# Identity transposes on TensorE in three idle stretches of a graph-attention kernel

## The chip, the cores and the metric

The kernel runs on 1 core of one Trainium2 chip. The metric is the device time of one execution in microseconds (us). A core has the matrix engine TensorE (PE), the vector engine VectorE (DVE), the activation engine ScalarE (ACT), GpSimd (POOL) and SyncE (SP), which here only issues transfers. Each engine works through its own instructions in order and waits on semaphores for the others.

## The reference

The input is x of 2048 x 512 and a sparse normalised adjacency matrix of 2048 x 2048. Cut to what matters:

```
h = relu(layernorm(x))
# layer 0: A = (adj + adj.T) / 2 + I, scaled on both sides by deg ** -0.5
y = (Coefficient2 @ A_norm) @ h      # here Coefficient2 is adj itself
x = x + y
h = relu(layernorm(x))
# layer 1: attention with 8 heads of width 64
Wh = einsum('nf,hfd->hnd', h, W)
e  = leaky_relu(e_src[:, :, None] + e_dst[:, None, :], 0.2), -9e15 where adj is 0
att = softmax(e); out = elu(att @ Wh), then four dense layers 512-256-128-256-512
x = x + out
```

The kernel computes adj @ (A_norm @ h) in two products of 2048 x 2048 by 2048 x 512, instead of making the 2048 x 2048 product first.

## The kernel before

There are three blocks, one after the other. Between two blocks all engines meet at a barrier, so nothing of a block starts before everything of the one ahead is done.

**The first product** (`smooth_features`) makes G = A_norm @ h. It runs over 32 steps: a step takes one tile of 128 rows of adj plus its transpose against half of the columns (1024 of them), and multiplies it with one tile of h. The numbers are 32-bit; to keep precision each operand is cut into a high and a low part, and `split_product` issues three matmuls for one product (L73, L74, L75), 128 x 128 against 128 x 512 each. A step has 8 column blocks, one for each bank of PSUM, so 24 matmuls. TensorE waits at the start of step s for `lo_ready` (DVE has cut the low part of the matrix tile) and for `x_ready` (DVE has cut the low part of the feature tile, L298, which needs the node degree and so both halves of the tile from memory). The first four steps (`EARLY`) use rows while they are still being loaded and summed. VectorE's and ScalarE's order in this stretch is written out by hand. `deg_ready` is counted by DVE: its first count is the degree of tile 0 (L322), three counts a tile. `ident` is the 128 x 128 identity matrix, which POOL makes in the first two microseconds.

**The second product and the projection** (`spread_and_project`) make adj @ G in two halves of 16 steps with the same 24 matmuls a step, then the layer norm, the product with W (L73 to L75 again, now with `w_hi` and `w_lo`), with transposes of the features by TensorE (L1016) ahead of it, and the attention terms e (L1040, L1050, L1055 are small TensorE operations at the end of this block).

**The attention and the dense layers** (`attend_and_finish`) handle 16 rounds (4 pairs of heads by 4 groups of 512 rows). A round r on TensorE (`sum_up`) is three phases of 64 matmuls of 260 columns each:

- `q_phase` for the first head: matmuls L1593 into four banks. It reads q, a 0/1 tile that DVE makes (L1278, one for each of 16 column tiles), and `parts`, the features times the attention factors, cut in high and low by ACT and POOL (L1410, L1512). It waits for `first_lo` (POOL) and `q_ready` (DVE).
- `m_phase`: matmuls L1617 with the mask that ACT converts (`take_mask`, L1391). In round 0 it waits first for `second_lo` (DVE, L1287). Its four output banks are 4, 5, 0 and 1, and banks 0 and 1 are those of the q phase just ended, so the third matmul waits until ACT has copied the q sums out (`take_q_sums`, L1397). ACT issues in order: in round 0 the sums stand behind eight masks (L1391).
- `q_phase` for the second head.

The change adds TensorE instructions at the head of each block: ahead of `products(0, ...)` in the first and in the second, and ahead of everything else in the attention block. The sequence on all other engines stays, except for one semaphore count that POOL adds behind making `ident`.

Of the kernel before, what the change touches and what calls it, by code (L numbers as in the profile page):

```python
# [37 lines left out]
P = 128  # L38
# [32 lines left out]
def split_product(pe, acc, hi, lo, rhs_hi, rhs_lo, first):  # L71

    pe.matmul(acc, hi, rhs_hi, start=first, stop=False, skip_group_check=True)  # L73
    pe.matmul(acc, hi, rhs_lo, start=False, stop=False, skip_group_check=True)  # L74
    return pe.matmul(acc, lo, rhs_hi, start=False, stop=True, skip_group_check=True)  # L75


def if_set(eng, flag):
# [23 lines left out]
def smooth_features(nc, bank, ident, G, rows, rows_loaded, x, adj, adj_t):  # L102
# [5 lines left out]
    with ExitStack() as ctx:  # L108
# [3 lines left out]
        def sem(name):  # L112
            return ctx.enter_context(nc.semaphore(name))
# [39 lines left out]
        ident_zeroed = sem("ident_zeroed")  # L153
# [10 lines left out]
        deg_ready = sem("l0_deg_ready")  # L164
# [40 lines left out]
        with nc.Block() as block:  # L205
# [406 lines left out]
            @block.gpsimd  # L612
            def _(p):
                p.memset(ident[:], 0.0).then_inc(ident_zeroed, 1)
                p.wait_ge(ident_zeroed, 1)
                p.affine_select(out=ident[:], in_=ident[:], compare_op=ALU.not_equal, fill=1.0, base=0,
                                pattern=[[-1, P]], channel_multiplier=1)

            @block.tensor
            def _(pe):  # L620
                pe.sem_inc(slot_free, 2)

                def products(s, b, early=None, first=False, last=False, bank_free=None):
                    pe.wait_ge(lo_ready, s + 1)
                    if early is None:
                        pe.wait_ge(x_ready, s - EARLY + 1)
                    else:
                        pe.wait_ge(x_ready, early + 1)
                    right = ((x_hi[:, b, :], x_lo[:, b, :]) if early is None
                             else (early_hi[:, early, :], early_lo[:, early, :]))  # L630
                    for k in range(G8):
                        if bank_free is not None:
                            pe.wait_ge(bank_free, k + 1)
                        cols = slice(k * P, (k + 1) * P)
                        mm = split_product(pe, bank[k][:], s_hi[:, b, cols], s_lo[:, b, cols], *right, first)
                        if last and k < G8 - 1:
                            mm.then_inc(acc_done, 1)
                    mm.then_inc(slot_free, 1)

                for s in range(EARLY):  # L640
                    products(s, s % 2, s, s == 0, s == EARLY - 1)
                for s in range(EARLY, FIRST_NOW):
                    products(s, s % 2, s - EARLY, s == EARLY, False, part_kept if s == EARLY else None)
                products(FIRST_NOW, 0)
                with pe.Fori(0, (FIRST_LATE - FIRST_NOW) // 2 - 1) as j:
                    products(FIRST_NOW + 1 + 2 * j, 1)
                    products(FIRST_NOW + 2 + 2 * j, 0)
                products(FIRST_LATE - 1, 1, last=True)
                products(FIRST_LATE, 0, first=True, bank_free=g_done)
                with pe.Fori(0, (STEPS - FIRST_LATE) // 2 - 1) as j:  # L650
                    products(FIRST_LATE + 1 + 2 * j, 1)
                    products(FIRST_LATE + 2 + 2 * j, 0)
                products(STEPS - 1, 1, last=True)


def in_turns(count, *stages):

    for k in range(count + max(lag for _, lag in stages)):
        yield k
        for work, lag in stages:  # L660
            if 0 <= k - lag < count:
                work(k - lag, (k - lag) % 2)


def spread_and_project(nc, bank, G, rows, rows_loaded, x1, mask, wh, e, fac, neg_d, ident, x, adj_t, w, a1, a2,
# [3 lines left out]
    with ExitStack() as ctx:  # L669
# [78 lines left out]
        with nc.Block() as block:  # L748
# [235 lines left out]
            @block.tensor  # L984
            def _(pe):
                pe.sem_inc(slot_free, 2)

                def products(s, b, g, first, last):
                    pe.wait_ge(g_ready, s + 1)
                    pe.wait_ge(lo_ready, s + 1)  # L990
                    for k in range(G8):
                        if first and g == 1:
                            pe.wait_ge(x1_done, k + 1)
                        cols = slice(k * P, (k + 1) * P)
                        mm = split_product(pe, bank[k][:], a_hi[:, b, cols], a_lo[:, b, cols],
                                           g_hi[:, b, :], g_lo[:, b, :], first)
                        if last:
                            mm.then_inc(acc_done, 1)
                    if not last:
                        mm.then_inc(slot_free, 1)  # L1000

                for g in range(2):
                    products(T * g, 0, g, True, False)
                    with pe.Fori(0, T // 2 - 1) as j:
                        products(T * g + 2 * j + 1, 1, g, False, False)
                        products(T * g + 2 * j + 2, 0, g, False, False)
                    products(T * g + T - 1, 1, g, False, True)
                    if g == 0:
                        pe.wait_ge(acc_done, G8)
                        pe.sem_inc(slot_free, 1)  # L1010

                def turn(t, b):
                    pe.wait_ge(h_ready, t + 1)
                    for k in range(KC):
                        cols = slice(k * P, (k + 1) * P)
                        mm = pe.transpose(bank[b][:, cols], h2[:, b, cols], ident[:])  # L1016
                    mm.then_inc(turned, 1)

                def project(t, b):
                    pe.wait_ge(t_lo_ready, t + 1)  # L1020
                    pe.wait_ge(wh_ready, t + 1)
                    for k in range(KC):
                        cols = slice(k * P, (k + 1) * P)
                        mm = split_product(pe, bank[2 + b][:], g_hi[:, b, cols], g_lo[:, b, cols],
                                           w_hi[:, k, :], w_lo[:, k, :], k == 0)
                    mm.then_inc(wh_summed, 1)

                pe.wait_ge(x1_done, G8 + 4)
                pe.wait_ge(w_ready, 1)
                pe.sem_inc(turned, 2)  # L1030
                pe.sem_inc(wh_summed, 2)
                def turn_e(tiles):
                    for t in tiles:
                        q = t // 4
                        if t % 4 == 0 and q >= 2:
                            pe.wait_ge(e_copied, q - 1)
                            pe.wait_ge(top_ready, q - 1)
                        if t % 4 == 0 or t >= OWN:
                            pe.wait_ge(e_ready, 2 * min(t + 4 - t % 4, max(t + 1, OWN)) + 4)
                        mm = pe.transpose(bank[4 + q % 2][0:2 * H, (t % 4) * P:(t % 4 + 1) * P], e[:, t, :], ident[:])  # L1040
                        if t % 4 == 3:
                            mm.then_inc(e_turned, 1)

                for k in in_turns(T, (turn, 0), (project, 1)):
                    if k in (8, 12, 16):
                        turn_e(range(k - 8, k - 4))
                pe.wait_ge(sel_ready, 2)
                pe.wait_ge(e_copied, 1)
                for hh in range(2):
                    pe.matmul(bank[6 + hh][:], sel[:, hh, :], e_t[:, 0:512], start=True, stop=True  # L1050
                              ).then_inc(src_spread, 1)
                turn_e(range(12, T))

                pe.wait_ge(top_ready, 6)
                pe.matmul(bank[0][:, 0:2 * H], top_w[:], ident[0:2 * H, 0:2 * H], start=True, stop=True  # L1055
                          ).then_inc(top_spread, 1)


def attend_and_finish(nc, bank, wh, e, mask, ident, adj, e_rows, fac, neg_d, wh_store, x1_store, weights, out):
# [10 lines left out]
    with ExitStack() as ctx:  # L1070
# [152 lines left out]
        with nc.Block() as block:  # L1223
# [352 lines left out]
            def _(pe):  # L1576
                pe.sem_inc(q_done, T)
                pe.sem_inc(m_done, T)

                def wait_for_bank(r, phase, t):  # L1580

                    if phase == 0:
                        pe.wait_ge((m_bank_free, q_bank_free)[t // 2], (GT * r + 3 + t, 2 * GT * r + t - 1)[t // 2])
                    elif phase == 1:
                        pe.wait_ge(q_bank_free, 2 * GT * r + 3 + t)
                    else:
                        pe.wait_ge((q_bank_free, m_bank_free)[t // 2], (2 * GT * r + 7 + t, GT * r + 3 + t)[t // 2])
# [512 lines left out]
```

## Time and profile before

| | |
|---|---|
| time, median of 3 runs | 918.83 us (916.86 to 919.87) |
| the profiled execution's own time | 916.54 us |
| its span, first to last instruction | 914.6 us |
| mean granted TensorE clock | 0.985 |
| TensorE busy (matmuls) | 859.8 us, 94% |
| VectorE busy | 691.7 us, 76% |
| ScalarE / GpSimd busy | 412.0 us / 275.2 us |

The span is 1.9 us shorter than the time of the same execution. TensorE's matmuls are pipelined: a record's duration is longer than the distance from one start to the next, and it is the distance that says how fast the engine goes.

TensorE's clock is granted at one of two levels, 1.2 and 2.4 GHz. The column PEclk of the windows gives it as a share of 2.4 GHz (0.50 is the lower level throughout). Ahead of the first change of level in the record, the column shows 1.00; what the level was in that stretch, the distance between matmuls has to tell.

### The profile page before, as it was taken

The page shows a single profiled execution, that of the slowest core. Times are in us where ns is not written, and L with a number is a line of the kernel's source. Part 1 is how long each engine was busy: PE and PEld are TensorE (multiplying, and loading weights), DVE is VectorE, ACT ScalarE, POOL GpSimd, SP SyncE. Part 2 cuts the span into 40 slices and gives each one's busy share as a digit, 9 for nine tenths or more (in the row PEclk, how much of TensorE's full clock was granted, in tenths as well). Part 3 has the DMA queues.
Part 4 walks back from the last instruction along what each step waited for, and adds up shares of the span by engine and source line. Part 5 has one row for each costly group of instructions (what it writes and reads, how often), then busy time and mean ns, then how long its engine had stood idle before and what let it go on. Part 6 is the DMA issues. An engine that isn't in the chain of part 4 may idle for free.

```text
span 914.6 us, 15458 instructions
## 1 busy us (share of the span) xinstructions
PE 859.8 (94%) x5144; PEld 753.6 (82%) x5144; DVE 691.7 (76%) x1199; ACT 412.0 (45%) x743; POOL 275.2 (30%) x287
## 2 busy tenths in 40 slices
PE   1899999989999999999599999999999999998997
PEld 1687888868888888778399999999999999997553
DVE  5688886554556875666899999999999999997622
ACT  2344433221212111245386666666666656774331
POOL 0000000000000000057646555555555545573111
PEclk9999999998999999999799999999999999999999
DMA  9949930009332222130051000000000022001132
GB/s 344 406 168 301 395 132 1 0 20 292 126 104 100 92 92 69 58 127 4 27 199 25 23 23 24 25 24 23 24 24 24 23 93 70 13 1 47 47 136 96
DMA packets 36131, 87.36 MB, mean 96 GB/s; under 512 B 7088, under 2 KB 7984, under 8 KB 36080
## 3 DMA queue, kind: packets, MB, share of 16 engines
q1 hardware_dynamic: 35040, 82.46, 26.2%
q0 software_dynamic: 1040, 4.26, 1.2%
q8 instruction: 27, 0.44, 0.2%
q14 instruction: 24, 0.20, 0.1%
HBM read 73.93 MB, written 12.78 MB: 95 GB/s over the span
## 4 chain that ended last, share of the span: by engine, by line
PE 45%; DVE 3%; POOL 1%; ACT 1%; issue 1%; ACTq 0%; POOLq 0%; DVEq 0%
PE bank L1593 24%; PE bank L1617 13%; PE bank L2046 3%; DVE l_q L1278 2%; PE bank L73 1%; PE bank L74 1%; PE bank L75 1%; PE bank L2029 1%; PE bank L2038 1%; PE bank L2008 1%; DVE wh L1959 0%; POOL l_parts L1512 0%; POOL l_o_q L1505 0%; ACT l_mask L1391 0%; POOL l_o_m L1524 0%
## 5 line engine op out<-in xcount | busy, mean ns | idle before, releaser
L1278 DVE SCALAR_TENSOR_TENSOR l_q<-bank,neg_d,mask 128x512 fp32r<-128x512 f32 x512 | 338.6, 741 | 28.3 <-PE bank L1593 27.4
L1593 PE MATMUL bank<-l_parts,l_q 128*128 128x260 f32 x2048 | 250.7, 284 | 8.3 <-DVE l_q L1278 8.3
L1593 PEld LDWEIGHTS bank<-l_parts,l_q 128*128 128x128 f32 x2048 | 248.3, 189 | 8.4 <-issue 8.4
L838 POOL TENSOR_TENSOR l_prod<-wh,l_a 128x512 f32<-128x512 f32 x30 | 36.6, 1239 | 407.2 <-ACT wh L808 406.4
L1391 ACT ACTIVATE l_mask<-mask 128x512 fp32r (+1 forms) x256 | 136.3, 619 | 0.2
L1617 PE MATMUL bank<-l_parts,l_mask 128*128 128x260 f32 x1024 | 129.0, 286 | 2.0 <-ACT l_o_q L1397 2.0
L1617 PEld LDWEIGHTS bank<-l_parts,l_mask 128*128 128x128 f32 x1024 | 127.1, 189 | 2.3 <-ACT l_o_q L1397 2.2
L73 PE MATMUL bank<-l_g_hi,l_a_hi 128*128 128x512 f32 x256 | 100.8, 394 | 4.5 <-DVE l_a_lo L856 4.2
L74 PE MATMUL bank<-l_g_lo,l_a_hi 128*128 128x512 f32 x256 | 100.6, 393 | 0.0
L75 PE MATMUL bank<-l_g_hi,l_a_lo 128*128 128x512 f32 x256 | 100.4, 392 | 0.0
L783 ACT ACTIVATE l_a_hi<-rows 128x1024 fp32r<-128x1024 f32 x32 | 33.9, 1062 | 147.2 <-PE bank L75 124.6
L1397 ACT ACTIVATE l_o_q<-bank 128x260 f32<-128x260 f32 x128 | 49.0, 388 | 104.9 <-PE bank L1593 96.9
L73 PE MATMUL bank<-l_x_hi,l_s_hi 128*128 128x512 f32 x192 | 74.9, 390 | 0.7 <-DVE l_x_lo L298 0.7
L75 PE MATMUL bank<-l_x_hi,l_s_lo 128*128 128x512 f32 x192 | 74.7, 389 | 0.0
L74 PE MATMUL bank<-l_x_lo,l_s_hi 128*128 128x512 f32 x192 | 74.7, 389 | 0.0
L73 PEld LDWEIGHTS bank<-l_g_hi,l_a_hi 128*128 128x128 f32 x256 | 48.7, 190 | 15.8 <-issue 5.7
L851 DVE CAST l_g_hi<-G 128x512 fp32r (+1 forms) x32 | 13.6, 426 | 61.6 <-PE bank L75 61.6
L75 PEld LDWEIGHTS bank<-l_g_hi,l_a_lo 128*128 128x128 f32 x256 | 48.6, 190 | 10.2
L74 PEld LDWEIGHTS bank<-l_g_lo,l_a_hi 128*128 128x128 f32 x256 | 48.6, 190 | 10.1
L73 PE MATMUL bank<-l_early_hi,l_s_hi 128*128 128x512 f32 x64 | 26.8, 418 | 22.2 <-DVE l_early_lo L298 22.2
L73 PEld LDWEIGHTS bank<-l_x_hi,l_s_hi 128*128 128x128 f32 x192 | 36.0, 188 | 9.0 <-DVE l_x_lo L298 1.5
L1212 POOL TENSOR_TENSOR l_o_m<-l_o_m 128x520 f32<-128x520 f32 x16 | 18.3, 1147 | 82.4 <-ACT l_o_m L1404 82.4
(176 smaller groups left out, 1241.1 us busy)
## 6 DMA issues: line engine op xcount, KB each, us to landing
rows<-adj_t SPq DMA_DIRECT2D x48, 512.0 KB, 4.1
l_now<-adj SPq DMA_DIRECT2D x16, 512.0 KB, 7.6
l_rows_k<-adj_t SPq DMA_DIRECT2D x16, 512.0 KB, 8.5
l_src<-e_rows SPq DMA_DIRECT2D x30, 256.0 KB, 3.2
l_kept<-adj SPq DMA_DIRECT2D x12, 512.0 KB, 12.7
wh_store<-wh POOLq DMA_DIRECT2D x1, 4160.0 KB, 14.3
x<-x SPq DMA_DIRECT2D x1, 4096.0 KB, 14.2
x_store<-x SPq DMA_DIRECT2D x1, 4096.0 KB, 12.8
```

Source lines behind the costliest of these rows:

```text
L73: pe.matmul(acc, hi, rhs_hi, start=first, stop=False, skip_group_check=True)
L74: pe.matmul(acc, hi, rhs_lo, start=False, stop=False, skip_group_check=True)
L75: return pe.matmul(acc, lo, rhs_hi, start=False, stop=True, skip_group_check=True)
L783: a.activation(a_hi[:, r % 2, :], rows[:, r, :], ACT.Copy).then_inc(hi_ready, 1)
L838: p.tensor_tensor(per_head(prod[:, b, n, :]), wh[:, t, :, 0:HD], per_head(a_b[:, n, :]), ALU.mult).then_inc(prod_ready, 1)
L1212: eng.tensor_tensor(m_hi, m_hi, m_lo, ALU.add).then_inc(summed, 1)
L1278: v.scalar_tensor_tensor(out=q[:, i, :], in0=bank[S_BANKS[hh]][:], scalar=neg_d[:, i, h:h + 1], in1=mask[:, i, cols], op0=ALU.is_ge, op1=A ...
L1391: a.activation(m_r[:, i % MR, :], mask[:, i, cols], ACT.Copy).then_inc(m_ready, 1)
L1397: a.activation(o_q[hh][:, t, :], bank[Q_BANKS[hh][t]][:, 0:PW], ACT.Copy).then_inc(q_bank_free, 1)
L1593: return pe.matmul(bank[Q_BANKS[hh][t]][:, 0:PW], q[:, i, t * P:(t + 1) * P], parts[pair_slot][:, hh, i, :], start=i == 0, stop=i == T - 1)
L1617: return pe.matmul(bank[M_BANKS[t]][:, 0:PW], m_r[:, i % MR, t * P:(t + 1) * P], parts[pair_slot][:, :, i, BOTH_C], start=i == 0, stop=i = ...
L2046: mm = pe.matmul(self.bank[self.ROW_BANKS[t % 2]][:], self.o3[:, c % 2, k, t * P:(t + 1) * P], self.w4_s[:, k, :], start=k == 0, stop=k == ...
```

## The change

A helper issues transposes of the identity matrix into a PSUM bank that nobody reads before it is overwritten. It is called at the head of the three blocks, with 28, 22 and 40 transposes. The call in the first block waits for `ident` and for the first count of `deg_ready`; the others follow the barrier at once. Each writes to a bank (7, 0 and 4) that a product of the same block starts afresh later.

```diff
+def keep_running(pe, acc, ident, count):
+    for k in range(count):
+        pe.transpose(acc[:, k % 4 * P:(k % 4 + 1) * P], ident[:], ident[:])
...
                 p.affine_select(out=ident[:], in_=ident[:], compare_op=ALU.not_equal, fill=1.0, base=0,
-                                pattern=[[-1, P]], channel_multiplier=1)
+                                pattern=[[-1, P]], channel_multiplier=1).then_inc(ident_zeroed, 1)
...
+                pe.wait_ge(ident_zeroed, 2)
+                pe.wait_ge(deg_ready, 1)
+                keep_running(pe, bank[7], ident, 28)
                 for s in range(EARLY):
                     products(s, s % 2, s, s == 0, s == EARLY - 1)
...
+                keep_running(pe, bank[0], ident, 22)
                 for g in range(2):
                     products(T * g, 0, g, True, False)
...
             def _(pe):
                 pe.sem_inc(q_done, T)
                 pe.sem_inc(m_done, T)
+                keep_running(pe, bank[4], ident, 40)
```

## Rows read from the trace of the kernel before

**Rows 1.** The page, part 2: busy tenths in 40 equal slices.

```profile
PE   1899999989999999999599999999999999998997
PEclk9999999998999999999799999999999999999999
```

**Rows 2.** TensorE's waits: line, tile, releaser: us in total, times, longest.

```profile
PE bank L73 <- DVE l_early_lo L298: 22.2, 2, 18.6
PE bank L1593 <- DVE l_q L1278: 8.3, 1, 8.3
PE bank L73 <- DVE l_a_lo L856: 4.2, 2, 3.9
```

**Rows 3.** Windows: from:to length, PE busy (x matmuls), PEclk, DMA share, GB/s.

```profile
35.00:40.00 5.00, 4.56 (x13) 0.67 1.04 397
...
400.00:405.00 5.00, 3.87 (x12) 0.69 0.00 0
...
456.83:459.80 2.97, 2.97 (x13) 0.50 0.00 0
...
500.00:600.00 100.00, 100.00 (x830) 1.00 0.08 22
```

**Rows 4.** TensorE's timeline, first product: start, length, operation [idle before].

```profile
18.63 0.76 PE L73 MATMUL bank<-l_early_hi,l_s_hi 128*128 128x512 f32 x1 [18.63 <-DVE l_early_lo L298]
...
23.03 0.40 PE L74 MATMUL bank<-l_early_lo,l_s_hi 128*128 128x512 f32 x1
23.26 0.40 PE L75 MATMUL bank<-l_early_hi,l_s_lo 128*128 128x512 f32 x1
...
35.44 0.47 PE L73 MATMUL bank<-l_early_hi,l_s_hi 128*128 128x512 f32 x1 [3.59 <-DVE l_early_lo L298]
...
36.67 0.62 PE L75 MATMUL bank<-l_early_hi,l_s_lo 128*128 128x512 f32 x1
```

**Rows 5.** VectorE's timeline, 12 to 30 us.

```profile
12.63 0.21 DVE L322 TENSOR_SCALAR l_deg<-l_part 128x1 f32<-128x1 f32 x1
...
28.17 1.23 DVE L308 SCALAR_TENSOR_TENSOR l_now<-rows,l_now 128x1024 f32<-128x1024 f32 x1 [1.40 <-DMA l_kept<-adj]
```

**Rows 6.** Timeline of all engines about the barrier ahead of the second product.

```profile
201.43 0.39 PE L75 MATMUL bank<-l_x_hi,l_s_lo 128*128 128x512 f32 x1
...
203.10 0.17 DVE L846 MEMSET wh<- 128x128 f32 x1 [0.49 <-PEq L205]
...
205.72 0.77 PE L73 MATMUL bank<-l_g_hi,l_a_hi 128*128 128x512 f32 x1 [3.90 <-DVE l_a_lo L856]
...
210.88 0.39 PE L73 MATMUL bank<-l_g_hi,l_a_hi 128*128 128x512 f32 x1
```

**Rows 7.** Timeline of all engines from the end of the projection.

```profile
444.30 0.49 PE L1040 MATMUL bank<-ident,e 128*16 128x128 f32 x3
...
450.68 10.62 DVE L1278 SCALAR_TENSOR_TENSOR l_q<-bank,neg_d,mask 128x512 fp32r<-128x512 f32 x16 [0.88 <-ACTq L1374]
...
456.83 9.32 PE L1593 MATMUL bank<-l_parts,l_q 128*128 128x260 f32 x64 [8.28 <-DVE l_q L1278]
...
463.97 1.23 DVE L1287 TENSOR_TENSOR l_parts<-l_whole,l_parts 128x1040 fp32r<-128x1040 f32 x1
...
467.94 1.19 ACT L1397 ACTIVATE l_o_q<-bank 128x260 f32<-128x260 f32 x4
468.36 8.02 PE L1617 MATMUL bank<-l_parts,l_mask 128*128 128x260 f32 x62 [1.97 <-ACT l_o_q L1397]
```

**Rows 8.** TensorE's timeline: transposes in the projection.

```profile
389.23 0.60 PE L1016 MATMUL bank<-ident,rows 128*128 128x128 f32 x4
...
400.58 0.66 PE L1016 MATMUL bank<-ident,rows 128*128 128x128 f32 x4 [1.58 <-ACT rows L803]
401.79 0.73 PE L73 MATMUL bank<-l_w_hi,l_g_hi 128*128 128x512 f32 x1 [0.55 <-DVE l_g_lo L915]
```

**Rows 9.** The identity tile's instructions: ns min/median/max, first and last start in us.

```profile
L1016 PE MATMUL bank<-ident,rows x64: 270/272/329, 383.4 to 436.2; 128*128 128x128 f32 x64
```

## The prediction

> **What bounds the kernel now.** I read the page's slices first [rows 1]. TensorE is at nine tenths nearly everywhere; the exceptions are the start, the slices about 201 us and 400 us, and slice 20 (about 445 to 457 us). The row under it, the clock, dips in the same places. So the kernel is bound by TensorE, and what it loses is of two kinds: waits, and stretches at the lower clock level behind them.
>
> The waits [rows 2] name the three stretches of this change: 18.6 us ahead of the first product, 3.9 us ahead of the second, 8.3 us ahead of the attention. What follows each is slow. From 205.72 to 210.88 stand 12 matmuls, 0.43 us each [rows 6]. In 456.83 to 459.80 it is 0.50, and 13 matmuls of 260 columns take 2.97 us, 0.228 us each, against 100 / 830 = 0.120 us each from 500 to 600 [rows 3]. At the start, from 18.63 to 23.03 stand 10 matmuls, 0.44 us each, and from 23.03 on they are 0.23 apart [rows 4]. So the first product starts at the lower level too. Two more low stretches have nothing to do with the change's places: 36.67 to about 40 us behind a wait of 3.59 us (clock 0.67 in the window from 35), and 401.79 to about 405 (0.69) [rows 3, 4, 8].
>
> A wait that stays and a clock that is high behind it would save the difference. Whether the end moves depends on what TensorE meets next, so I take the three places one by one.
>
> **What a transpose costs.** Four in a row (L1016) show 0.60 us [rows 8] where one record is 0.27 us long [rows 9], so they start (0.60 - 0.27) / 3 = 0.11 us apart, at the high level. At the low level no row shows them. Below they cost 0.11 as at the high one; above I double that, 0.22, because the other matmuls go from 0.23 to 0.44 and from 0.120 to 0.228 (times 1.9). I take 0.21, since a transpose is a matmul by its record.
>
> **First product, 28 transposes.** They start when DVE has the first degree, 12.63 + 0.21 = 12.84 [rows 5]. They take 28 x 0.11 = 3.1 us to 28 x 0.21 = 5.9 us, so they end between 16.0 and 18.8; the first matmul is at 18.63 now. At worst it is 0.2 us late. At best its 10 slow matmuls go at 0.23, and TensorE has done steps 0 and 1 by 10 x 0.21 = 2.1 us sooner. But then it waits for x of step 2, until 35.44 [rows 4]. That wait ends with DVE's L298 [rows 4], and in DVE's order L308 at 28.17 stands ahead of it, which waited for a transfer (kept<-adj) and not for TensorE [rows 5]; the transfers run at a share above 1.0 [rows 3]. So all 2.1 us go into the wait, which grows from 3.59 to 5.7 us. What is late next is the clock. Now it falls at 36.67, 1.23 us into step 2, with 5 matmuls done at high pace. After a longer idle it is likely low already at 35.44. In 1.23 us only 2.8 matmuls fit instead of 5: 2.2 x 0.23 = 0.5 us lost, and from 35.44 to 201.43 TensorE has no longer wait, so this passes to the end. Bounds: 0 (the clock falls at the same moment) to +0.5. I take +0.5.
>
> **Second product, 22 transposes.** The engines are past the barrier at 203.10, where DVE has its first instruction [rows 6]. TensorE's first matmul is at 205.72, so there are 2.6 us of room. At the high level the 22 take 22 x 0.11 = 2.4 us and end at 205.5: they fit, by 0.2 us. The 12 matmuls from 205.72 to 210.88 take 5.16 us now and would take 12 x 0.23 = 2.76: a gain of 2.4 us. Of TensorE's waits for DVE's operands in this product (L856), 4.2 us in 2, this one is 3.9 [rows 2]: DVE keeps up everywhere else, nothing becomes the bound, and the gain passes on. Bounds: -2.4 to the loss of the second rival.
>
> **Attention, 40 transposes.** The block begins at 450.68 [rows 7]. The 40 take 4.4 to 8.4 us and end between 455.1 and 459.1; the first matmul is at 456.83. If they bring the clock up on their way, some run at each pace, and they end close to 456. Then the 13 slow matmuls save 13 x (0.228 - 0.120) = 1.4 us. That gain is covered as well. The q phase ends at 465 instead of 466.4, and behind it the m phase can't start before DVE's L1287 (463.97 + 1.23 = 465.2), and its third matmul not before ACT has copied the sums at 467.94; ACT has eight masks ahead of them in its queue, whose start goes back to POOL and not to TensorE. So TensorE goes on at 468.36 as now [rows 7]: 0 us. The price, if that cover turns on us, is again the clock: a first idle of 1.97 us becomes one of about 3.2 us, broken by two matmuls. The clock has fallen behind 1.59 + 0.55 us with four transposes between [rows 8] and did not fall behind 1.97. If it falls, it stays low for 3.4 us (36.67 to 40) to 5.2 us (205.72 to 210.88), in which 15 to 23 matmuls at 0.228 take the place of those at 0.120: a loss of 3.4 x (1 - 0.120/0.228) = 1.6 to 2.5 us. Bounds: 0 to +2.5. The likeliest case takes 0.
>
> **Sum.** +0.5 - 2.4 + 0 = -1.9 us against the profiled execution's 916.54 (span 914.6 and 1.9 around it), 914.6. That execution lies 2.3 us under the median of the runs, and the clock's falls explain a spread of such a size: each is worth 1.6 to 2.5 us, and which idle triggers one seems to be near an edge. Against the median I forecast 918.83 - 1.9 = 916.9, said as 917.0.
>
> **The rivals.** All against the median.
>
> 1. *The clock falls behind the attention's first q phase* in most executions, because the idle there is longer: -1.9 + 2.0 (the middle of 1.6 to 2.5) = +0.1, 918.9. For it: the idle of 2.1 us and four transposes at 399 to 401.8 was enough. Against it: 1.97 us was not, and the kernel before may well pay here too in other executions.
>
> 2. *Transposes don't hold or raise the clock*; this is the case on the other side, slower. The rows allow it: four of them at 400.58 did not prevent the fall at 401.79 [rows 8], and the three of L1040 from 444.30 stand ahead of the low start of the attention [rows 7]. Its price is in the second product: the level falls at some 204 us, perhaps 8 of the 22 run at 0.11 and 14 at 0.21, 3.8 us together, end 206.9, so the first product is 1.2 us late. It decides from the point where the 22 take more than 2.6 us, 0.12 us each. The rise of the clock stays bound to the matmuls: if it comes at the same 210.88, 2.8 slow matmuls fewer are done by then, 0.6 us; if it moves along, more is lost, up to 1.9 us (22 at 0.21 from 203.1 are done at 207.7, 2.0 late). In the attention the q phase starts at 459.1 and ends 2.3 us later than 466.4, against 1.97 us of cover: +0.3. Together +0.9 to +2.2: about 920.3.
>  The Trainium skill, "TensorE: Matmul & The Clock Gate", Part 4 (PE-mode transpose), says just this: in transpose mode the higher clock level doesn't engage, since it does not count as the engine being busy in the same way. By that rule the forecast would be this rival's. The rows here neither confirm nor refute it, because in none of them do transposes stand alone for long.
>
> 3. *More is gained*: the shifted program also spares the low stretch at 401.79 (12 matmuls of it, about 3.4 x 0.47 = 1.6 us) in most executions, or the 0.5 us of the first product are not lost, or the kernel before usually pays at 468 and the new one doesn't: 914.5 to 915.5.
>
> 4. *The first product's 2.1 us pass through.* Against it stands the transfer wait at 28.17; 914.8 if it were so. Small.
>
> **How the numbers follow.** My forecast gets 0.44, rival 1 0.18, rival 2 0.18, rivals 3 and 4 together 0.20. Within 0.3% is 2.75 us, about what a measurement of this kernel can tell: 916.1 to 921.6. The forecast lies in its lower part and gives a quarter of its chance to faster (0.11), rivals 3 and 4 most of theirs (0.15), rival 1 next to none: 0.26. Slower by over 0.3% needs the worst of rival 2 and of rival 1 together: 0.05. The range goes from rival 3's 914.2 to rival 2's 920.5.
>
> **What would show each step.** 28, 22 and 40 matmuls of 128 columns on the helper's line, 0.11 us apart where the clock is 1.00. The first product: distances of 0.23 from the first matmul, the same 35.4 for step 2, with 5.7 us of wait ahead of it. The second: first matmul still 2.6 us behind the barrier, clock 1.00 in the next 5 us. The attention: q phase shorter by 1.4 us, and the third L1617 at the same distance of 17.7 us from the block's start; then the clock of the 5 us behind it, which tells my forecast from rival 1. If the 22 transposes are 0.2 apart, rival 2 holds. The prediction is wrong if TensorE waits longer anywhere in the second product or the round behind it.

## The result and the profile after

The changed kernel takes 921.99 us, the median of 12 runs (919.46 to 924.87), against 917.65 us of the kernel before in the same rounds. The ratio is 1.0052 (95% interval 1.0038 to 1.0066): slower by 0.5%, about 4.3 us at the medians. I had forecast 917.0 us with 0.69 for no change and 0.05 for slower; the median of before that I counted from was 918.83, 1.2 us above the one measured here. The profiled execution has a span of 923.0 us, 8.4 us over the one of before; its own time, 924.85, is near the upper end of the runs, as that of before was below its median, so the two traces differ by more than the medians do.

The page of the changed kernel, part 2, in the slices of [rows 1]:

```profile
PE   4799999998999999999789999999999999998997
PEclk9999999999899999989889999999999999999999
```

Counted from one, slice 10 (208 to 231 us) has fallen to 8 on TensorE, and the clock dips in slices 11, 18, 20 and 21.

TensorE's waits, with the columns of [rows 2] (the inserted lines shift the line numbers: L856 is L866 now, L1617 is L1629):

```profile
PE bank L73 <- DVE l_early_lo L305: 5.2, 2, 4.3
PE bank L73 <- DVE l_a_lo L866: 3.4, 1, 3.4
...
PE bank L1629 <- ACT l_o_q L1408: 2.4, 1, 2.4
```

The waits of 18.6, 8.3 and 3.9 us are gone, because transposes stand in them. The 3.4 us for l_a_lo look like what is left of the 3.9, and are not: they stand 25 us further on.

Windows of the changed kernel, with the columns of [rows 3]. The first two and the sixth and seventh hold transposes alone (the first one's 1.00 is that of a stretch without a record; its 27 starts in 5.76 us, 0.213 apart, are the low level):

```profile
12.42:18.18 5.76, 5.76 (x27) 1.00 1.03 406
202.47:205.08 2.61, 2.59 (x22) 1.00 0.60 151
205.08:210.00 4.92, 4.92 (x22) 1.00 0.98 350
230.46:236.00 5.54, 5.54 (x13) 0.50 0.59 194
390.30:393.60 3.30, 3.30 (x9) 0.50 1.04 386
455.31:458.50 3.19, 3.19 (x15) 0.50 0.36 130
458.50:461.40 2.90, 2.90 (x27) 1.00 0.11 40
472.96:478.90 5.94, 5.94 (x27) 0.50 1.02 381
```

In all three stretches the transposes did what they are there for. From 455.31 to 458.50 they start 3.19 / 15 = 0.213 us apart, then the level rises with nothing but transposes running, and they go at 2.90 / 27 = 0.107. The second product starts at the high level: 22 matmuls in 4.92 us, where [rows 6] had 12 in 5.16. But there are two low stretches of some 6 us each where the trace of before is high, from 230.46 and from 472.96, and a shorter one at 390.30. The timeline of TensorE and, below it, ScalarE and VectorE of the changed kernel shows the first:

```profile
205.08 0.47 PE L73 MATMUL bank<-l_g_hi,l_a_hi 128*128 128x512 f32 x1
...
230.46 0.77 PE L73 MATMUL bank<-l_g_hi,l_a_hi 128*128 128x512 f32 x1 [3.35 <-DVE l_a_lo L866]
```

```profile
228.00 1.06 ACT L793 ACTIVATE l_a_hi<-rows 128x1024 fp32r<-128x1024 f32 x1 [10.67 <-DMA rows<-adj_t]
229.09 1.23 DVE L866 TENSOR_TENSOR l_a_lo<-rows,l_a_hi 128x1024 fp32r<-128x1024 f32 x1 [6.12 <-ACT l_a_hi L793]
```

TensorE waits 3.35 us ahead of step 4 of the second product, the first step whose rows are not yet loaded at the barrier. VectorE waits for ScalarE, ScalarE 10.67 us for the transfer of the rows. SyncE's queue says why it is late:

```profile
202.25 0.38 SPq L762 DMA_DIRECT2D x<-x  x1
202.67 15.49 SPq L764 DMA_DIRECT2D l_w<-w  x4
218.21 1.40 SPq L768 DMA_DIRECT2D l_a<-a  x2
220.03 14.25 SPq L94 DMA_DIRECT2D rows<-adj_t  x6
```

The first row tile is issued at 220.03, behind x (4 MB), W and the attention vectors, although its slot in memory was free long before: in the run with the rows first, below, the same tile is issued at 205.54. It is also slow to land while x and W are on their way: 8.4 us from issue to landing here (median of six), 4.2 us in the trace of rows_first. How much of the delay is the place in the queue and how much the shared transfer no run separates; both come from the order. The trace of before has the same queue:

```profile
217.90 1.62 SPq L758 DMA_DIRECT2D l_a<-a  x2
219.94 14.28 SPq L87 DMA_DIRECT2D rows<-adj_t  x6
```

There TensorE came to this point at 230.12 and waited 0.3 us, the other one of the two waits in [rows 2] (4.2 in 2, longest 3.9). (My expectations below call this wait "ahead of step 5", counting the steps from one.)

The attention of the changed kernel, the lines that answer to [rows 7]:

```profile
455.24 10.63 DVE L1289 SCALAR_TENSOR_TENSOR l_q<-bank,neg_d,mask 128x512 fp32r<-128x512 f32 x16 [0.88 <-ACTq L1385]
...
461.43 7.94 PE L1605 MATMUL bank<-l_parts,l_q 128*128 128x260 f32 x64
...
470.04 0.50 PE L1629 MATMUL bank<-l_parts,l_mask 128*128 128x260 f32 x2 [0.67 <-ACT l_mask L1402]
...
472.96 10.51 PE L1629 MATMUL bank<-l_parts,l_mask 128*128 128x260 f32 x62 [2.41 <-ACT l_o_q L1408]
```

The q phase is 1.4 us shorter by its length (7.94 for 9.32), and the third matmul of the m phase starts 472.96 - 455.24 = 17.7 us after the block, as before (468.36 - 450.68 = 17.7). The 62 matmuls behind it take 10.51 us instead of 8.02.

Setting one timeline beside the other shows where the traces part. Each row is a start that both have.

| TensorE's start of | before | after | shift |
|---|---|---|---|
| first product | 18.63 | 18.23 | -0.4 |
| second product | 205.72 | 205.08 | -0.6 |
| its step 4 | 230.40 | 230.46 | +0.1 |
| projection, first matmul | 386.36 | 389.31 | +2.9 |
| attention block (VectorE) | 450.68 | 455.24 | +4.6 |
| m phase, third matmul | 468.36 | 472.96 | +4.6 |
| second q phase | 476.22 | 483.31 | +7.1 |
| third group of feature transposes | 833.15 | 840.22 | +7.1 |
| end of the span | 914.6 | 923.0 | +8.4 |

Three microseconds come between step 4 and the projection, 2.5 in the m phase. The other two steps, 1.6 us behind 389 and 1.3 behind 840, are falls of the clock behind waits of 1.95 and 2.35 us that both kernels have. Such falls come in one execution and not in another: from the projection's first matmul to the attention block it is 62.9 us in four of the 17 profiles with those waits as they were, 64.3 to 64.5 in nine and 65.9 in four, and no kind of kernel has all of one sort. So the some 3 us of these two steps are chance, and the runs' medians differ by less than the traces.

### The profile page after: what moved, and what is told of

The parts are those of the page before. It is cut to its first block, busy times and chain, and to the rows that moved or that the text cites. A ratio compares the mean times of both kernels' runs of the same rounds, so it can differ in the third digit from the quotient of the medians.

```text
span 923.0 us, 15639 instructions
## 1 busy us (share of the span) xinstructions
PE 877.5 (95%) x5234; PEld 770.4 (83%) x5234; DVE 691.1 (75%) x1199; ACT 412.7 (45%) x743; POOL 275.1 (30%) x287
## 4 chain that ended last, share of the span: by engine, by line
PE 45%; DVE 2%; POOL 1%; ACT 1%; issue 1%; ACTq 0%; POOLq 0%; DVEq 0%
PE bank L1605 25%; PE bank L1629 13%; PE bank L2058 3%; DVE l_q L1289 2%; PE bank L73 1%; PE bank L75 1%; PE bank L74 1%; PE bank L2041 1%; PE bank L2050 1%; PE bank L2020 1%; DVE wh L1971 0%; POOL l_parts L1523 0%; POOL l_o_q L1516 0%; ACT l_mask L1402 0%; POOL l_o_m L1535 0%
## 5 line engine op out<-in xcount | busy, mean ns | idle before, releaser
L1629 PE MATMUL bank<-l_parts,l_mask 128*128 128x260 f32 x1024 | 131.5, 290 | 3.1 <-ACT l_o_q L1408 2.4
L1629 PEld LDWEIGHTS bank<-l_parts,l_mask 128*128 128x128 f32 x1024 | 129.6, 193 | 3.5 <-ACT l_o_q L1408 2.6
L866 DVE TENSOR_TENSOR l_a_lo<-rows,l_a_hi 128x1024 fp32r<-128x1024 f32 x32 | 39.1, 1222 | 6.1 <-ACT l_a_hi L793 6.1
```

The costliest lines, as they stand in the source:

```text
L866: v.tensor_tensor(a_lo[:, b, :], rows[:, r, :], a_hi[:, b, :].bitcast(F32), ALU.subtract).then_inc(lo_ready, 1)
L1629: return pe.matmul(bank[M_BANKS[t]][:, 0:PW], m_r[:, i % MR, t * P:(t + 1) * P], parts[pair_slot][:, :, i, BOTH_C], start=i == 0, stop=i = ...
```

## The experiments

Each line gives the median, the median of before in the same rounds, and the ratio with its interval. The shorthand is 28/22/40 for the transposes ahead of the first product, the second, and the attention.

| run | transposes | other edit | us | before | ratio |
|---|---|---|---|---|---|
| only_first | 28/0/0 | | 917.12 | 917.41 | 0.9989 (0.9977 to 1.0001) |
| only_second | 0/22/0 | | 919.06 | 917.41 | 1.0013 (0.9997 to 1.0029) |
| only_third | 0/0/40 | | 919.99 | 917.41 | 1.0013 (0.9994 to 1.0031) |
| second_rows_first | 0/22/0 | rows first | 914.23 | 917.41 | 0.9959 (0.9941 to 0.9978) |
| rows_first | none | rows first | 915.30 | 917.65 | 0.9980 (0.9965 to 0.9996) |
| third_filled | 0/0/40 | 32 behind q | 917.85 | 917.65 | 1.0004 (0.9991 to 1.0016) |
| three_rows_first_filled | 28/22/40 | both | 915.67 | 917.65 | 0.9984 (0.9974 to 0.9993) |
| second_q16_rows_first | 0/22/0 | rows first, 18 behind q | 914.55 | 917.65 | 0.9964 (0.9950 to 0.9978) |
| changed_again | 28/22/40 | | 921.77 | 917.35 | 1.0058 (1.0037 to 1.0079) |
| three_rows_first | 28/22/40 | rows first | 916.90 | 917.35 | 0.9996 (0.9982 to 1.0010) |
| three_filled | 28/22/40 | 32 behind q | 920.47 | 917.35 | 1.0038 (1.0023 to 1.0052) |
| waits_filled | 0/22/0 | rows first, five waits filled | 911.75 | 917.35 | 0.9941 (0.9920 to 0.9962) |
| first_second | 28/22/0 | | 920.73 | 917.06 | 1.0043 (1.0026 to 1.0060) |
| second_third | 0/22/40 | | 923.63 | 917.06 | 1.0071 (1.0049 to 1.0094) |
| first_third | 28/0/40 | | 919.81 | 917.06 | 1.0028 (1.0011 to 1.0044) |
| second_again | 0/22/0 | | 918.82 | 917.06 | 1.0025 (1.0009 to 1.0041) |

**One stretch at a time.** Each is the changed kernel with the other two calls left out, as here for the second:

```diff
-                pe.wait_ge(ident_zeroed, 2)
-                pe.wait_ge(deg_ready, 1)
-                keep_running(pe, bank[7], ident, 28)
...
-                keep_running(pe, bank[4], ident, 40)
```

> Only the 28 transposes ahead of the first product. Theory of the sum (each stretch is costly by what follows it, not by the transposes): the first product starts at the same time and at the high level, the wait ahead of step 2 (3.6 us) grows by about 2 us, and the rest is as before: -0.6 to +0.5 us, no change that can be told. Rival (the time is lost by clock falls anywhere, each stretch a share alike): about +1.4 us.

> Only the 22 transposes ahead of the second product. Theory: the 2.4 us that the faster start gives end in a wait of 2 to 3.5 us ahead of step 5, for the row tiles whose transfers stand in SyncE's queue behind those of x and W, and the clock falls behind that wait for 3.4 to 6.8 us: +1.5 to +3.0 us against before. Rival (the step in my prediction: nothing else becomes the bound): -2.4 us. Second rival (a share alike): +1.4 us.

> Only the 40 transposes ahead of the attention. Theory: the q phase is 1.4 us shorter, the third matmul of the m phase starts no sooner after the block's start (17.7 us), and behind the idle of over 3 us with two matmuls in it the clock is low for 3.4 to 6.8 us: +1.6 to +2.5 us in most executions. Rival (the fall is chance and no more frequent than before): 0 us. Second rival (a share alike): +1.4 us, without a fall of the clock at this place.

The first alone changes nothing that can be told. Its trace starts the first product at the high level, then waits 1.1 us ahead of step 1, and the wait ahead of step 2 has grown from 3.59 to 4.27 us.

The trace of the second alone repeats what the changed kernel showed. TensorE's timeline and its windows, columns as before:

```profile
230.92 0.77 PE L73 MATMUL bank<-l_g_hi,l_a_hi 128*128 128x512 f32 x1 [3.00 <-DVE l_a_lo L862]
```

```profile
225.00:230.00 5.00, 2.91 (x13) 1.00 0.90 317
230.00:235.00 5.00, 4.08 (x10) 0.50 0.52 192
```

The trace of the third alone has the wait in the m phase and the low level behind it, 16 matmuls of 260 columns in 3.00 us:

```profile
468.07 2.17 PE L1624 MATMUL bank<-l_parts,l_mask 128*128 128x260 f32 x13 [2.39 <-ACT l_o_q L1403]
```

```profile
470.00:473.00 3.00, 3.00 (x16) 0.50 1.02 380
```

Both losses are in the traces, and the step of my prediction that would have given -2.4 us for the second (a ratio of 0.9974) lies outside its interval. The ratios of the two alone are small, and whether each is a loss could not be said from them.

**Is it the order of the transfers?** SyncE issues the rows of steps 4 to 7 first, then x, W and the vectors, then the rest:

```diff
-                sp.dma_start(x1[:], x.rearrange("(t p) f -> p t f", p=P)).then_inc(x_loaded, 16)
...
-                for g in range(2):
-                    with sp.Fori(1 - g, T // SLOTS) as j:
+                load_rows(0, (1, 2))
+                load_features_and_weights()
+                load_rows(0, (2, T // SLOTS))
+                load_rows(1, (0, T // SLOTS))
```

> The 22 transposes ahead of the second product, and SyncE issues the four row tiles of steps 4 to 7 ahead of x, W and the two attention vectors instead of behind them. Theory: no wait ahead of step 5, no fall of the clock there, so the gain of 2.4 us (and the 0.3 us wait of before) reaches the end: -2 to -3 us against before. Rival (the loss is due to the transposes or to the clock's chance, not to the order of transfers): +1.4 to +3 us as with the transposes alone.

> The kernel before with SyncE's order changed alone: row tiles of steps 4 to 7 ahead of x, W and the attention vectors; no transposes. It is the control of the run with both. Theory: it removes only the wait of 0.3 us ahead of step 5: -0.3 us, the same. Rival (the order is worth something by itself, through memory or issue time): -1 us or more, and then the run with both owes its gain to it.

The same 22 transposes that cost with the old order are part of a kernel that is 0.4% faster with the new one. Windows of that kernel (second_rows_first):

```profile
205.00:210.00 5.00, 4.99 (x22) 1.00 0.45 134
225.00:230.00 5.00, 5.00 (x24) 1.00 1.04 372
230.00:235.00 5.00, 5.00 (x23) 1.00 1.10 360
```

TensorE is busy throughout, and the clock is high. So the loss was not the transposes' but that of the late rows. The traces say it without the noise of the falls further on. From VectorE's first instruction past the barrier to the projection's first matmul it is 183.0 to 184.3 us in the five with the old order and no transposes there, and 184.8 to 186.8 in the seven with the 22. With the rows first it is 182.6 in the one without transposes and 180.4 to 181.7 in the five with them. The 22 cost with the one order and gain with the other, and no trace of one kind falls among those of another.

The control brought a miss: the order alone was to give 0.3 us and gave 0.20%, 1.8 us (interval 0.4 to 3.2). The reason is in the traces of the kernels with the old order and no transposes ahead of the second product. They wait at the same step for 0.3 us (before), 2.05 (only_first), 0.8 (only_third), 1.1 (third_filled) and 1.0 (first_third), always until 230.0 to 231.3. In only_first the start behind the 3.9 us wait had 12 matmuls from 205 to 210, against 10 of before, so it lost less there; it reached the step earlier and waited longer:

```profile
205.00:210.00 5.00, 4.35 (x12) 0.66 1.02 379
```

```profile
231.33 0.47 PE L73 MATMUL bank<-l_g_hi,l_a_hi 128*128 128x512 f32 x1 [2.05 <-DVE l_a_lo L865]
```

With the old order step 4 starts at about the same time whatever TensorE does ahead of it: 27.3 to 28.6 us behind SyncE's first transfer of the block in all twelve profiles, with the 22 transposes and without. The low stretch that I set out to save cost the kernel before nearly nothing. With the rows first, the 22 transposes are worth 0.9959 against 0.9980, some 0.2% or 1.9 us, near my 2.4; the two intervals overlap, and it is the 1 to 2 us in the traces above that support it. The bound was moved, not removed: in four of the six traces with the rows first TensorE waits 0.3 to 1.1 us ahead of step 8, whose rows now stand behind x and W.

**Is it the idle time in the m phase?** 32 transposes go between the first q phase and the m phase of round 0; TensorE's first four rounds are written out instead of looped for it:

```diff
                     q_phase(r, pair_slot, 0)
+                    if isinstance(r, int) and r == 0:
+                        keep_running(pe, bank[4], ident, 32)
                     pe.wait_ge(second_lo, 2)
```

> The 40 transposes ahead of the attention, and 32 more in the idle time between the first q phase and the m phase of round 0 (about 3.5 us at the high level; TensorE's loop over the first four rounds is written out for it). Theory: the third matmul of the m phase starts at the same 17.7 us after the block's start, the clock stays high behind it, and the 1.6 to 2.5 us are not lost: 0 to -0.8 us against before (which falls there in some executions too). Rival (the fall there is chance, or the time is lost otherwise): the same loss as with the 40 alone.

> All three groups of transposes, and 32 more between the first q and m phases; the transfers in the order of before. Theory: the m phase's 2.5 us are not lost, those behind step 5's wait are: 1.5 to 2.5 us under the changed kernel, still 1 to 3 us above before. Rival: no change against the changed kernel.

TensorE's timeline and windows of third_filled:

```profile
465.61 3.65 PE L81 MATMUL bank<-ident 128*128 128x128 f32 x32
469.02 8.09 PE L1624 MATMUL bank<-l_parts,l_mask 128*128 128x260 f32 x64
```

```profile
470.00:475.00 5.00, 5.00 (x43) 1.00 1.01 379
```

No fall, and all 64 matmuls in 8.09 us. The fill ends a little late: the m phase starts at 469.02, some 0.5 us behind the point where its third matmul could, and so the 40 and the 32 together are worth nothing against before (1.0004). In the full changed kernel the fill takes 1.0058 to 1.0038, 1.3 us at the medians and 1.8 by the ratios, in the direction and near the size expected, though the two intervals overlap.

The traces are sharper than the medians here too. From the block's start (VectorE's first q tile) to the second q phase it is 25.5 to 25.6 us in all nine without the 40, with or without a short fill. It is 27.1 in three of the six with the 40 and no fill (only_third, first_third, three_rows_first), 28.1 in the other three, and 25.6 to 26.1 in the three with the fill. So the 40 save nothing and cost 1.5 or 2.5 us, and filling the idle time takes 1 to 2.5 us of it back.

**All parts, mended.**

> All three groups of transposes, and SyncE's row tiles ahead of x and W; nothing between the q and m phases. Theory: the second stretch's loss is gone and turned to a gain, the third's is still there: -2.5 + 1.5 to 2.5, so -1 to 0 us against before, 3 to 5 us under the changed kernel. Rival (order of the transfers does not matter once all three are in): as the changed kernel.

> The changed kernel with both mends: the row tiles ahead of x and W, and 32 transposes between the first q and m phases. Theory: the sum of parts, 0 (first) - 2.5 (second) - 0.4 (third): about -2.5 us against before, 7 us under the changed kernel. Rival: if the parts do not add, it stays within 1 us of before.

> No transposes ahead of the first product and of the attention; the 22 ahead of the second with the row tiles first, and 18 (2.0 us) between the first q and m phases, where the kernel before is idle for 2.0 us. Theory: -2.4 - 0.3 (second) and, as the clock cannot fall behind the q phase in any execution, up to -1 more: -2.5 to -3.5 us. Rival: -2.5 as the second stretch alone gives.

The rows first take the changed kernel from 1.0058 to 0.9996, 4.9 us by the medians: that is the loss behind step 4 and the gain that becomes free. With both mends it is 0.9984, 1.5 us under before where I had expected 2.5. The second stretch with 18 transposes behind the q phase is 0.9964, no better than without (0.9959). I had expected up to 1 us; but in the trace of second_rows_first that wait is 0.8 us and no fall follows, so there was nothing to save.

**Do the parts add?**

> The changed kernel once more, as it stands, beside the three below on the same chip. Its first timing gave ratio 1.0052, while the three parts alone gave 0.9989, 1.0013 and 1.0013, which add up to 1.0015. Theory (the stretches act one by one): about 1.0015 to 1.003. Rival (the parts together cost more than alone, since each shifts where the clock falls later on): 1.005 again.

> Transposes ahead of the first and the second product (28 and 22), none ahead of the attention. If the stretches act one by one: the second's loss alone, 1.001 to 1.002. If the first worsens what the second brings (a later fall of the clock in the first product, or a longer wait ahead of step 5): about 1.004.

> Transposes ahead of the second product and the attention (22 and 40). One by one: 1.003 (0.0013 + 0.0013, or up to 0.0018 + 0.0028 by the medians). If these two interact: 1.005 as all three.

> Transposes ahead of the first product and the attention (28 and 40). One by one: 1.0002 to 1.002, the third's loss alone. If these two interact: 1.003 or more.

> The 22 transposes ahead of the second product alone, once more. If its first value was low by chance: about 1.003, near what its trace lost (3 us). If the first value holds: 1.001.

The first three singles add up to +0.15%, the three together give +0.52% and +0.58%. Of what I had written ahead, the repeated kernel (1.0058) and the three pairs (1.0043, 1.0071, 1.0028) all came out near or above the figures for an interaction, not near those for stretches that act one by one. But the latter had been added up from the first values of the singles, and the second stretch, timed again, gave 1.0025 for its 1.0013 (the intervals overlap). Fitting one value for each stretch to all nine ratios (weighted by their intervals) gives -0.02% for the first, +0.29% for the second and +0.27% for the third, each within 0.1%, with residuals up to 0.16%, a bit more than the intervals allow. So the changed kernel's +0.54% can be read as the sum of the second and third, about 2.7 and 2.4 us. An interaction is not excluded: a term for one pair, added to the fit, comes out at 0.04 to 0.15% and uncertain by 0.2%.

The traces do show one of about 1 us in the attention. In the four with the 22 transposes, the old order and the 40 (the two of the changed kernel, second_third and three_filled) the level rises sooner and the 40 take 6.0 to 6.1 us. In the other five with the 40 they take 6.9 to 7.3 us, and the q phase starts 0.6 to 1.0 us later than it could. Three of the first four have no fill. There the q phase ends sooner, TensorE waits 0.7 us once more ahead of the wait of 2.4, and the loss is 2.5 us instead of 1.5. Why the level rises sooner there stays open.

**A version that beats both.** From second_rows_first I went on to the waits that are left, with transposes in each (in this order: ahead of the first projection, ahead of the transposes of tile 5 and of the projection of tile 4, between the first q and m phases, ahead of the third group of feature transposes, and ahead of the dense layers):

```diff
+                    if t == 0:
+                        keep_running(pe, bank[2], ident, 17)
...
+                        pe.wait_ge(x1_done, T)
+                        keep_running(pe, bank[7], ident, 13)
...
+                        keep_running(pe, bank[7], ident, 4)
...
+                        keep_running(pe, bank[4], ident, 17)
...
+                        if i == 10:
+                            keep_running(pe, bank[0], ident, 20)
...
+                keep_running(pe, bank[0], ident, 8)
```

> A version to beat both: 22 transposes ahead of the second product with the row tiles first, none ahead of the first product or the attention, and transposes in the waits that are left: 17 ahead of the first projection, 13 and 4 about tile 5's, 17 between the first q and m phases, 20 ahead of the third group of transposes of the features and 8 ahead of the dense layers. Theory: from 40 us to the end the clock falls only once, ahead of the attention, where it is covered; each fall that goes (about 1.5 us, at 385, 401, 468 and 831, in a half of the executions each) is a gain: -4.5 to -7 us against before. Rival (filling a wait exactly makes TensorE late where the fill is too long, and costs as much): -3 us, as with the second stretch alone.

It takes 911.75 us (7 runs), 5.6 us or 0.6% under before and 10 us under the changed kernel, as expected (4.5 to 7 us). What the five waits alone are worth over second_rows_first (0.9959) or second_q16_rows_first (0.9964) is not clear of noise, as the intervals overlap. The clock is low in one stretch only, ahead of the attention. Its page, part 2:

```profile
PE   1899999999999999999599999999999999999997
PEclk9999999999999999999799999999999999999999
```

## Why the prediction was wrong

**What a transpose costs: right.** 0.107 us at the high level and 0.213 at the low one; I had 0.11 and 0.21.

**Rival 2, that transposes don't hold or raise the clock: refuted.** The level rose during transposes alone, ahead of the first matmul at 18.23 and again at about 458.5, and it did not fall over the 22 ahead of the second product. The Trainium skill's sentence on transpose mode ("TensorE: Matmul & The Clock Gate", Part 4) does not hold for these transposes of 32-bit numbers; the measurement decides.

**First product: right, and near nothing.** The gain did go into waits for the same loads, in two parts: 0.9 us ahead of step 1, which I had missed, and 0.7 more ahead of step 2 (5.2 us in two waits, longest 4.3, in the changed kernel). The 0.5 us that I charged for the clock behind it can be neither seen nor excluded: the fit gives -0.02% with 0.09%, or 0.8 us, to either side.

**Second product: this step failed.** I wrote that "DVE keeps up everywhere else, nothing becomes the bound, and the gain passes on", with a term of -2.4 us. The saving at the start was real (22 matmuls from 205 to 210 where the five traces without the transposes have 10 to 13), but 25 us later stands a transfer whose time is fixed by its place behind x and W in SyncE's queue. The term was 0 at best, and the wait that took its place, 2.6 to 3.7 us in the seven profiles that have the 22 transposes and the old order, was followed by a low clock in all seven. It did so in none of the five profiles with the old order and no transposes there, whose waits were 0.3 to 2.05 us. So the term came out at +0.29%, 2.7 us, and the sign that I had set for being wrong, a longer wait in the second product, is what the trace showed. My evidence was [rows 2] itself: 4.2 us in two waits, the longest 3.9. I took the remaining 0.3 us as proof that nothing else is near. It was the opposite: a point where TensorE just touched the next bound, and every microsecond gained ahead of it would be waited there.

**Attention: this term was mis-set too, though its mechanism was named.** The gain of 1.4 us was covered by ScalarE's queue as I said (17.7 us both times), and the price of a fall was right (1.6 to 2.5 us said; 1.5 us in three traces, 2.5 in the other three, 2.4 by the fit). I took 0 as likeliest and gave the fall 0.18, because 1.97 us of idle time had not caused it. In the six profiles with the 40 transposes and nothing behind the q phase, the wait was 2.4 us (in three of them with one of 0.7 us shortly ahead), and the clock fell in all six; in the seven without the 40 and without a fill, with waits of 0.8 to 2.0 us, in none. The 32 transposes in that idle time took the fall away. So at this place what decided was how long TensorE stands, and making the stretch ahead faster lengthens just that. It is no rule for other places: the wait of 1.95 us ahead of the projection was followed by a fall in the changed kernel's trace and not in that of before.

My sum was +0.5 - 2.4 + 0; the fit gives 0 + 2.7 + 2.4. Rival 1's fall of the clock came, but its 918.9 still counted on the -2.4. No rival had a loss behind the start of the second product, so the range ended at 920.5, 1.5 us short. "Slower by over 0.3%" had 0.05 and happened.

## What to carry to other kernels

A stretch made faster arrives earlier at the next wait, and on TensorE, as here, that can cost twice, once as the wait and once as the low clock behind it: find the next point where the engine waits at all, however little, and what fixes its time, before counting a gain. A wait of 0.3 us on the bounding engine was here a bound just touched, not slack. Transposes of the identity did keep the clock up. They can pay in waits that nothing can shorten, if they end when the real work is ready, and if nothing behind swallows the gain.

## What was not expected of the hardware

Transposes of a 128 x 128 identity of 32-bit numbers, with nothing else on TensorE, brought the granted clock from 0.50 to 1.00 and their own distance from 0.213 to 0.107 us. And the start of step 4 of the second product, which comes 27.3 to 28.6 us behind SyncE's first transfer with either kernel, hid whether TensorE had run at the low clock for 3 us (only_third), for 5 (before) or not at all ahead of it; the work saved there came back as a longer wait.
